# A graph network on one core: one expansion product a slot, scores ahead of the next maxima, messages at once, and a joined unpacking stage

## The chip, the cores and the metric

The kernel runs on one core of a Trainium2 chip. The number that counts is the device time of one execution in microseconds (us). Before the change the median of three runs is 8563.55 us (8562.0 to 8572.29).

## The reference, cut to what matters

Four layers run over a graph of 6250 nodes and 106250 edges, each followed by a residual and a layer norm. The change touches the first two layers.

```python
x = _layernorm(x + _L0_gnn_ref(x, ...), axis=-1)     # relation messages: sum of x[src] @ W[type] per target
x = _layernorm(x + _L1_gnn_ref(x, edge_index, ...))  # first attention
x = _layernorm(x + _L2_gnn_ref(x, edge_index, ...))  # second attention
x = _layernorm(x + _L3_gnn_ref(x, edge_index))       # routing, 6 rounds

# L1, HEADS = 4, HID = 64
h = (x @ W).reshape(n, HEADS, HID)
a_src = einsum('nhf,hf->nh', h, att_src);  a_dst = einsum('nhf,hf->nh', h, att_dst)
e = leaky_relu(a_src[src] + a_dst[dst], 0.2)
m = segment_max(e, dst, n)
ex = exp(e - m[dst])
alpha = ex / segment_sum(ex, dst, n)[dst]
agg = segment_sum(h[src] * alpha[:, :, None], dst, n)
out = relu(agg.reshape(n, HEADS * HID) + bias) @ fc_w + fc_b
```

## The kernel before, in words

Nodes lie in 49 tiles of 128. Edges are sorted on the chip into chunks of 128 slots, each chunk belonging to one target tile; there are NCH = 880 chunks, and 464 pairs of chunks (NPAIR) of which the last ones are padding that reads one same dummy row. The program is a row of phases, and between two phases stands a barrier of all engines. In each phase every engine runs its own instruction list, and semaphores order the engines.

**Start.** Tables `y_tab` are made, and GpSimd (POOL) scatters one record an edge (L296).

**Unpacking phase (L534 to L574).** SyncE (SP) loads all records into `rec` by one DMA (L546). VectorE (DVE) unpacks three columns, `dl_f` (lane of the target), `y_row` (row of `y_tab`) and `src_row`; TensorE (PE) turns `dl_f` in seven blocks, DVE copies them to `dl_t`, and SP stores that to `dl_tab`. A barrier follows.

**First pass (L694 on).** DVE clears the whole of `acc` (13000 elements a partition) and `ring`, and copies `lane` to PSUM. Only then does POOL gather rows of `y_tab`, one indirect DMA a chunk (L584), four chunks (a quad) a ring slot, four slots. PE multiplies each chunk by a one-hot matrix (`hots`, made by DVE, L652), and DVE adds the product to `acc` (L785). DVE also makes byte tables of the one-hot matrices from `dl_b`, which SP loads from `dl_tab` (L731) and stores again for the later passes.

**dense_layer (twice).** It normalizes the sums, multiplies by `fc`, adds, runs the layer norm and writes the table of the next pass. In the second call SP loads four slots of own rows (L937, 512 KB each) first, then `fc`, `h_col`, `fcb_b` and the table weights. PE waits for these weights (`s_fc`) ahead of `turn(0)`, its first transposes; `turn(g)` also waits for POOL's product of own rows `g` (`s_oh`, L1088).

**attend_running (first attention pass).** It goes over 58 places of 16 chunks (8 pairs). For each place POOL issues 16 gathers of table rows into one of three ring slots (L1356); a slot is free when the totals of the place three before have been made. The other engines work in a pipeline over two places; E is the start of the exponential of a place (ScalarE, ACT, L1557):

- maxima of place b: PE spreads the source scores of a pair (`spread`, 8 matmuls, L1626), DVE reduces them (`reduce`, L1402, 1024 elements) and takes the running maximum (`top`, L1410). Eight pairs a place. The spreads of pairs 0 to 3 need `line(b, 0)`, those of pairs 4 to 7 `line(b, 1)`, which ACT copies (L1536) from PE's `turn(b, n)` (L1612) of ACT's `pack(b, n)` (L1527).
- `shift(b)`: four DVE instructions (L1416 to L1424) make the new shift of every node, in three bf16 parts.
- `expand(b)`: PE brings target score and shift to the edges: for each of 16 chunks three accumulating matmuls of 8 columns, one a part, so 48 (L1637).
- `scores(b)`: three DVE instructions (L1455, L1458, L1461). Then ACT's two exponentials (L1557 to PSUM, L1558), then DVE's `message(b)` for one head (L1467) and ACT's `message(b, a)` for three heads (L1566, 6 instructions a pair).
- `total(b, a)`: PE sums a pair (L1654) and DVE adds it to `acc` (L1475), one place later, between the maxima of the next place.

DVE's order around a place: reduces and tops of b with adds of b-1; `shift`; the last two adds of b-1; `reduce(b+1, 0)`, `reduce(b+1, 1)` and `top(b+1, 0)`; `scores(b)`; `message(b)`; `rescale(b)` (L1443, L1446). ACT's order: exponentials of b-1; `pack(b, 1)`; `line(b, 1)`, which waits for PE's turn; the 48 message instructions of b-1; `pack(b+1, 0)`; `hot(b)`; `line(b+1, 0)`; `widen(b+1)`; `fading(b)`; exponentials of b.

## Time and profile before

| | |
|---|---|
| median of three runs | 8563.55 us |
| profiled execution, device time | 8565.55 us |
| its span in the profile | 8563.6 us |
| busy: PE, DVE, ACT, POOL | 62%, 66%, 36%, 71% of the span |
| unpacking phase and start of the first pass | 1183 to 1222 us |
| first pass | 1222 to 2353 us |
| first dense layer | 2353 to 2455 us |
| first attention pass | 2455 to 3716 us |
| second dense layer | from 3716 us |

The profile gives, for one execution, busy and idle time by engine and by group of instructions, and what released each wait. Shares over the whole span mix stages with different limits, so the stages are read one by one, in the view in order of time. Granted clock is the TensorE clock as a share of 2.4 GHz; 0.50 is the 1.2 GHz level.

### The profile page before, as it was taken

To read this page: it belongs to the slowest core of one execution; us is meant where nothing else is said; L and a number is where in the kernel's file an instruction comes from. 1 tells how busy PE (TensorE), PEld (TensorE's weight loads), DVE (VectorE), ACT (ScalarE), POOL (GpSimd) and SP (SyncE) were. 2 spreads that over 40 slices of the span, in tenths; PEclk is the share of its full clock that TensorE was granted. 3 is DMA by queue.
4 is the path that set the end of the run, shared out by engine and by line. 5 is a ranking of instruction groups with operands and counts; after the bars stand their busy time and mean duration, and the time that the engine had idled before them with its cause. 6 is when DMAs were issued, how large, how long until landed. Compare 5 with 4: busy or idle time off the path is not lost. (4 is left out here: it accounts for less than half of the span.)

```text
span 8563.6 us, 137030 instructions
## 1 busy us (share of the span) xinstructions
PE 5287.4 (62%) x37370; PEld 4671.1 (55%) x37370; DVE 5613.1 (66%) x13450; ACT 3042.1 (36%) x7001; POOL 6100.7 (71%) x5620
## 2 busy tenths in 40 slices
PE   0991014444368888763444415655579898989896
PEld 0340013333346666563333315655579898989896
DVE  9661025555578888763444455555579898989898
ACT  2000002000048888732222222222256666666564
POOL 4777767777647777727777727777768787878785
PEclk6995555555578888886666657677689999999998
DMA  1771015565645555623333324444567676767674
GB/s 43 271 308 54 2 46 130 131 145 131 118 111 139 138 136 138 123 66 79 82 79 82 79 48 130 129 129 130 123 172 221 189 222 190 222 189 222 189 222 138
DMA packets 962997, 1176.44 MB, mean 137 GB/s; under 512 B 286474, under 2 KB 845278, under 8 KB 949198
## 3 DMA queue, kind: packets, MB, share of 16 engines
q1 hardware_dynamic: 806638, 864.50, 33.2%
q0 software_dynamic: 155616, 303.19, 16.6%
q8 instruction: 326, 5.34, 0.3%
q14 instruction: 417, 3.42, 0.1%
HBM read 897.16 MB, written 269.96 MB: 136 GB/s over the span
## 5 line engine op out<-in xcount | busy, mean ns | idle before, releaser
L2572 PE MATMUL ps<-u,wide_r 128*128 x9280 | 1141.9, 277 | 128.7 <-issue 89.0
L2572 PEld LDWEIGHTS ps<-u,wide_r 128*128 128x128 f32 x9280 | 1093.6, 194 | 130.7 <-issue 130.7
L2147 POOL DMA_INDIRECT z_r<-x_tab,src_row x880 | 852.6, 969 | 417.5 <-issue 267.8
L2584 PE MATMUL ps<-msg_r,hots_r 128*128 128x128 f32 x9280 | 1135.5, 275 | 21.5 <-POOL msg_r L2405 21.5
L2405 POOL TENSOR_TENSOR msg_r<-zo_r,share_r 128x1024 f32<-128x1024 f32 x580 | 1123.1, 1936 | 11.8 <-DVE share_r L2457 9.0
L1356 POOL DMA_INDIRECT ring_e<-t_tab,src_p x928 | 878.9, 947 | 322.7 <-issue 269.7
L2584 PEld LDWEIGHTS ps<-msg_r,hots_r 128*128 128x128 f32 x9280 | 1082.6, 192 | 26.7 <-POOL msg_r L2405 25.3
L296 POOL DMA_INDIRECT rec_tab<-pay,row_i x831 | 806.3, 970 | 375.0 <-issue 274.3
L584 POOL DMA_INDIRECT ring<-y_tab,y_row x880 | 839.4, 954 | 306.0 <-issue 266.2
L2413 POOL TENSOR_TENSOR prod_r<-prod_r 128x512 f32<-128x512 f32 x580 | 735.0, 1267 | 415.9 <-DVE prod_r L2435 414.6
L1767 POOL DMA_INDIRECT ring_e<-t_tab,src_row x880 | 830.7, 944 | 271.9 <-issue 271.9
L843 PE MATMUL ps<-ring,hots 128*128 128x129 f32 x1760 | 453.2, 438 | 696.9 <-issue 548.2
L843 PEld LDWEIGHTS ps<-ring,hots 128*128 128x128 f32 x1760 | 394.1, 329 | 756.1 <-issue 649.9
L2289 PE MATMUL ps<-unit,wide_r 128*128 x1760 | 398.0, 418 | 582.9 <-ACT wide_r L2254 582.9
L2468 DVE TENSOR_TENSOR u_sum<-ps,u_sum 128x128 f32 x2320 | 670.9, 289 | 91.7 <-PE ps L2584 17.8
L2435 DVE TENSOR_TENSOR prod_r<-ps,zo_r 128x1024 f32<-128x1024 f32 x580 | 704.5, 1215 | 35.7 <-PE ps L2572 32.4
L2289 PEld LDWEIGHTS ps<-unit,wide_r 128*128 128x128 f32 x1760 | 369.5, 320 | 603.1 <-issue 603.1
L1566 ACT ACTIVATE ring_e<-ring_e 128x64 f32<-128x64 f32 x2752 | 662.2, 335 | 0.0
L2518 ACT ACTIVATE wide_r<-zo_r 128x1024 f32<-128x1024 uint8 x580 | 605.4, 1044 | 96.2 <-PE ps L2572 62.6
L1654 PE MATMUL ps<-ring_e,hots_e 128*128 128x260 f32 x1856 | 580.7, 446 | 81.1 <-ACT ring_e L1566 54.7
L1402 DVE TENSOR_REDUCE high_e<-ps 128x4 f32<-128x1024 f32 x464 | 559.6, 1216 | 69.1 <-PE ps L1626 65.4
L2535 ACT ACTIVATE hots_r<-zo_r 128x1024 f32<-128x1024 uint8 x580 | 603.3, 1040 | 0.0
(320 smaller groups left out, 9520.7 us busy)
## 6 DMA issues: line engine op xcount, KB each, us to landing
zo_r<-zo_tab SPq DMA_DIRECT2D x2320, 192.0 KB, 2.8
y_tab<-wide SPq DMA_DIRECT2D x100, 1024.0 KB, 3.9
zo_tab<-z_r SPq DMA_DIRECT2D x110, 512.0 KB
hot_bytes_e<-hb_tab SPq DMA_DIRECT2D x464, 64.0 KB
dl_b<-dl_tab SPq DMA_DIRECT2D x220, 128.0 KB, 3.8
zo_tab<-hot_bytes SPq DMA_DIRECT2D x220, 128.0 KB, 2.3
hb_tab<-hot_bytes SPq DMA_DIRECT2D x220, 128.0 KB, 2.3
hot_bytes_e<-hb_tab SPq DMA_DIRECT2D x55, 512.0 KB
```

The source lines that it names most:

```text
L296: nc.gpsimd.indirect_dma_start(out=rec_tab, out_offset=bass.IndirectOffsetOnAxis(ap=row_i[:, j:j + 1], axis=0), in_=pay[:, j, :], in_offse ...
L584: nc.gpsimd.indirect_dma_start(out=ring[:, s, c, 0:width], out_offset=None, in_=table, in_offset=bass.IndirectOffsetOnAxis(ap=rows[:, q * ...
L843: last = nc.tensor.matmul(sum_of(s, c), hots[:, s, c, :], ring[:, s, c, :], start=True, stop=True)
L1356: nc.gpsimd.indirect_dma_start(out=ring[:, b % ZR, c, :], out_offset=None, in_=t_tab, in_offset=bass.IndirectOffsetOnAxis(ap=src_p[:, b * ...
L1767: nc.gpsimd.indirect_dma_start(out=ring[:, b % ZR, c, :], out_offset=None, in_=t_tab, in_offset=bass.IndirectOffsetOnAxis(ap=src_row[:, b ...
L2147: nc.gpsimd.indirect_dma_start(out=z[:, g % ZR, c, :], out_offset=None, in_=x3_tab, in_offset=bass.IndirectOffsetOnAxis(ap=src_row[:, g * ...
L2289: last = nc.tensor.matmul(ps[:, 2 * (g % 2) + c // 4, c % 4 * D:(c % 4 + 1) * D], wide[:, g % WR, c, :], unit[:, bass.ds(tiles[at // CQ, a ...
L2405: nc.gpsimd.tensor_tensor(msg[:, g % WR].rearrange("p c (k d) -> p c k d", d=CD), z_of(g).rearrange("p c (k d) -> p c k d", d=CD), share[: ...
L2413: nc.gpsimd.tensor_tensor(prod[:, :, 0:CD // 2], prod[:, :, 0:CD // 2], prod[:, :, CD // 2:CD], ALU.add).then_inc(s_half, 1)
L2435: v.tensor_tensor(prod[:].rearrange("p (c k) d -> p c (k d)", k=CAPS), up, z_of(g), ALU.mult).then_inc(s_prod, 1)
L2572: last = nc.tensor.matmul(ps[:, 2 * (g % 2) + c // 4, c % 4 * D:(c % 4 + 1) * D], wide[:, g % WR, c, :], u[:, bass.ds(tiles[g % NO % 4 * O ...
L2584: last = nc.tensor.matmul(ps[:, 4 + g % 2, c // 2 * D:(c // 2 + 1) * D], hots[:, g % WR, c, :], msg[:, g % WR, c, :], start=c % 2 == 0, st ...
```

## The change

Four things are edited. (1) The unpacking phase is gone as a phase: its instructions move into the first pass. `rec` is loaded in two DMAs, columns 0 to 63 and the rest, and POOL's gather waits for `y_row` of the first 64 columns only (and at quad 16 for the rest) in place of the clearing. DVE clears the last column of `ring` and the first 129 columns of each `acc` tile only, behind the unpacking. (2) In the first attention pass `expand` is one matmul of 24 columns a chunk, and DVE adds the three parts in a new reduce into `sent` ahead of the scores. (3) There DVE's order becomes `scores(b)`, `reduce(b+1, 0)`, `message(b)`, `rescale(b)`, `reduce(b+1, 1)`, `top(b+1, 0)`; ACT starts the messages of b-1 right behind the exponentials, with `pack(b, 1)` ahead of pair 1 and `line(b, 1)` ahead of pair 2; PE's `turn(b, 1)` moves behind `total(b-1, 0)`. (4) In the dense layers `turn(0)` stands ahead of the wait for the first weights, and in the second call own rows 1 to 3 are loaded behind `fc`, `h_col` and `fcb_b`.

```diff
-        with Phase() as ph:
-            rec = sb("rec", [P, NCH, 4], i32, ph)
...
-                    sp.dma_start(rec[:], rec_tab[0:SLOTS, :].rearrange("(p c) w -> p c w", p=P)).then_inc(s_r, 16)
...
                 @block.sync
                 def _(sp):
+                    for n, c in enumerate((slice(0, FIRST), slice(FIRST, NCH))):
+                        sp.dma_start(rec[:, c, :], rec_tab[0:SLOTS, :].rearrange("(p c) w -> p c w", p=P)[:, c, :])\
+                          .then_inc(s_r[n], 16)
+                    sp.wait_ge(s_d, BL)
+                    for b in range(BL):
+                        rows = min(P, NCH - b * P)
+                        sp.dma_start(dl_tab[b * P:b * P + rows, :], dl_t[0:rows, b, :]).then_inc(s_o, 16)
+                    sp.wait_ge(s_o, 16 * BL)
...
                 def _(pool):
-                    pool.wait_ge(s_ini, 2)
-                    gather = gather_quads(pool, y_tab, y_row, ring, s_gath, s_sum, D)
+                    gather_rows = gather_quads(pool, y_tab, y_row, ring, s_gath, s_sum, D)
+
+                    def gather(q, s):
+                        if q % (FIRST // CQ) == 0 and q <= FIRST // CQ:
+                            pool.wait_ge(s_y, q // (FIRST // CQ) + 1)
+                        gather_rows(q, s)
...
                 def _(dve):
-                    nc.vector.memset(acc[:], 0.0).then_inc(s_ini, 1)
-                    nc.vector.memset(ring[:], 1.0).then_inc(s_ini, 1)
+                    nc.vector.memset(dl_t[:], 0.0).then_inc(s_z, 1)
+                    nc.vector.memset(ring[:, :, :, D:W], 1.0).then_inc(s_ini, 1)
                     nc.vector.tensor_copy(lane_ps, lane[:]).then_inc(s_ini, 1)
+                    for n, c in enumerate((slice(0, FIRST), slice(FIRST, NCH))):
+                        dve.wait_ge(s_r[n], 16)
+                        nc.vector.tensor_copy(y_row[:, c], rec[:, c, 0]).then_inc(s_y, 1)
+                    nc.vector.tensor_copy(dl_f[:], rec[:, :, 2]).then_inc(s_c, 1)
+                    nc.vector.tensor_copy(src_row[:], rec[:, :, 1]).then_inc(s_c, 1)
+                    nc.vector.memset(acc[:, :, 0:W], 0.0).then_inc(s_ini, 1)
...
                     if not first:
-                        for g in range(OR):
-                            own_in(g)
+                        own_in(0)
                     sp.dma_start(fc[:], fc_in.rearrange("(k d) n -> d k n", d=P)).then_inc(s_fc, 16)
...
+                        for g in range(1, OR):
+                            own_in(g)
...
+                    turn(0)
                     if first:
                         pe.wait_ge(s_wr, 1)
                     else:
                         pe.wait_ge(s_fc, 64)
-                    turn(0)
...
+                            v.tensor_reduce(sent[:].rearrange("p c w -> p (c w)"),
+                                            expanded(b).rearrange("p (c k w) -> p c w k", c=BC, k=3),
+                                            AX.X, ALU.add).then_inc(s_sent, 1)
...
-                            if b + 1 < NB:
-                                reduce(b + 1, 0)
-                                reduce(b + 1, 1)
-                                top(b + 1, 0)
...
                             if now:
                                 scores(b)
+                            if b + 1 < NB:
+                                reduce(b + 1, 0)
+                            if now:
                                 message(b)
                                 if behind:
                                     rescale(b)
+                            if b + 1 < NB:
+                                reduce(b + 1, 1)
+                                top(b + 1, 0)
...
-                            if b < NB:
-                                pack(b, 1)
-                                line(b, 1)
-                            if b >= 1:
-                                for a in range(BP):
+                            for a in range(BP):
+                                if b < NB and a == 1:
+                                    pack(b, 1)
+                                if b < NB and a == 2:
+                                    line(b, 1)
+                                if b >= 1:
                                     message(b - 1, a)
...
                             for c in range(BC):
-                                for k in range(3):
-                                    last = nc.tensor.matmul(
-                                        sent_of(b)[:, c, :], wide[:, b % WR, c, :],
-                                        sent_b[:, b % 2, bass.ds(tiles[b][c // 2], 1), k, 1:4 * HEADS:2]
-                                        .rearrange("p t w -> p (t w)"), start=k == 0, stop=k == 2)
+                                last = nc.tensor.matmul(
+                                    expanded(b)[:, c * SW:(c + 1) * SW], wide[:, b % WR, c, :],
+                                    sent_b[:, b % 2, bass.ds(tiles[b][c // 2], 1)]
+                                    .rearrange("p t k w -> p (t k w)")[:, 1:2 * SW:2], start=True, stop=True)
...
-                                    if a == 2:
+                                    if a == 3:
                                         turn(b, 1)
```

## Rows read from the trace of the kernel before

**Rows 1.** Page: busy, mean ns, idle before (part 5); KB, us to landing (6).
```profile
L584 POOL DMA_INDIRECT ring<-y_tab,y_row x880 | 839.4, 954 | 306.0 <-issue 266.2
...
zo_r<-zo_tab SPq DMA_DIRECT2D x2320, 192.0 KB, 2.8
```
**Rows 2.** In order of time, unpacking phase; start, duration (us), idle before in brackets.
```profile
1189.55 0.33 SPq L546 DMA_DIRECT2D rec<-rec_tab  x1
1196.58 0.94 DVE L558 CAST dl_f<-rec 128x880 f32<-128x880 int32 x1 [6.44 <-DMA rec<-rec_tab]
...
1205.78 1.28 SPq L731 DMA_DIRECT2D dl_b<-dl_tab  x3
1208.56 10.89 DVE L759 MEMSET acc<- 128x13000 f32 x1 [7.91 <-issue]
...
1221.88 0.97 POOL L584 DMA_INDIRECT ring<-y_tab,y_row  x1 [37.88 <-DVE ps L761]
```
**Rows 3.** The line of the gathers of the first attention pass; idle before it.
```profile
L1356 POOL DMA_INDIRECT ring_e<-t_tab,src_p x928: 940/946/1140, 2455.4 to 3639.8; - x186
...
  issue: 269.7, 885
  PE ps L1654: 36.7, 42
```
**Rows 4.** In order of time, one place of that pass.
```profile
2989.58 0.23 ACT L1557 ACTIVATE ps<-score_e 128x64 f32<-128x64 f32 x1 [2.83 <-DVE score_e L1461]
...
2990.93 11.55 ACT L1566 ACTIVATE ring_e<-ring_e 128x64 f32<-128x64 f32 x48
...
2992.51 2.10 PE L1654 MATMUL ps<-ring_e,hots_e 128*128 128x260 f32 x4 [0.93 <-ACT ring_e L1566]
...
2995.50 1.23 DVE L1402 TENSOR_REDUCE high_e<-ps 128x4 f32<-128x1024 f32 x1 [0.32 <-PE ps L1626]
...
3003.55 0.37 DVE L1416 TENSOR_TENSOR sum_n_e<-most,a_dst 128x200 f32<-128x200 f32 x1
...
3006.31 2.93 PE L1637 MATMUL ps<-sent_n_e,wide_e 128*128 x48
...
3006.82 2.34 DVE L1402 TENSOR_REDUCE high_e<-ps 128x4 f32<-128x1024 f32 x2
...
3010.04 0.23 ACT L1557 ACTIVATE ps<-score_e 128x64 f32<-128x64 f32 x1 [2.80 <-DVE score_e L1461]
```
**Rows 5.** In order of time, second attention pass: its expansion and its reduce.
```profile
3920.34 1.76 PE L1908 MATMUL ps<-exp_n_e,wide_e 128*128 x16
3922.14 0.37 DVE L1787 TENSOR_REDUCE ps<-ps 128x64 f32<-128x192 f32 x1 [2.35 <-PE ps L1908]
...
4040.97 0.93 PE L1908 MATMUL ps<-exp_n_e,wide_e 128*128 x16
```
**Rows 6.** In order of time, end of the first attention pass.
```profile
3573.16 0.94 POOL L1356 DMA_INDIRECT ring_e<-t_tab,src_p  x1 [0.85 <-PE ps L1654]
...
3656.83 1.87 PE L1626 MATMUL ps<-lines_e,pick_e 104*128 104x128 bf16 x16 [30.65 <-issue]
...
3661.61 0.23 ACT L1557 ACTIVATE ps<-score_e 128x64 f32<-128x64 f32 x1 [33.13 <-DVE score_e L1461]
...
3682.15 0.23 ACT L1557 ACTIVATE ps<-score_e 128x64 f32<-128x64 f32 x1 [2.68 <-DVE score_e L1461]
...
3702.24 0.23 ACT L1557 ACTIVATE ps<-score_e 128x64 f32<-128x64 f32 x1 [4.08 <-DVE score_e L1461]
```
**Rows 7.** Stretches: us, busy (instructions) of PE, PEld, DVE, ACT, POOL; clock, DMA share, GB/s.
```profile
3630.00:3640.00 10.00, 0.00 (x0) 0.00 (x0) 0.00 (x0) 0.00 (x0) 7.56 (x9) 0.50 1.02 97
```
**Rows 8.** In order of time, starts of the two dense layers.
```profile
2361.48 1.94 PE L1168 MATMUL ps<-ident,acc 128*128 128x128 f32 x8 [12.04 <-DVE acc L986]
3720.09 4.49 POOL L1088 TENSOR_TENSOR own_rows_d<-own_rows_d,own 128x1024 f32<-128x1024 f32 x1 [15.43 <-DMA own_rows_d<-t_tab]
3725.65 0.79 PE L1170 MATMUL ps<-ident,acc 128*128 128x128 f32 x2 [11.12 <-DMA fcb_b_d<-in_L_gnn_fc_b]
```

More of the change, by code:

```diff
@@ L705, in gnn_resnorm_kernel @@
             s_bst = [sem(f"hot_bytes_stored_0_{s}", ph) for s in range(RING)]
+            FIRST = 64
+            rec = sb("rec", [P, NCH, 4], i32, ph)
+            s_r = [sem(f"records_in_{n}", ph) for n in range(2)]
+            s_y = sem("y_rows_unpacked", ph)
+            s_c = sem("records_unpacked", ph)
+            s_z = sem("target_rows_cleared", ph)
+            s_t = sem("dl_transposed", ph)
+            s_d = sem("dl_rows_ready", ph)
+            s_o = sem("dl_rows_stored", ph)
             dl_i = sb("dl_i_0", [P, BL, P], i32, ph)
@@ L758, in _ @@
                 def _(dve):
-                    nc.vector.memset(acc[:], 0.0).then_inc(s_ini, 1)
-                    nc.vector.memset(ring[:], 1.0).then_inc(s_ini, 1)
+                    nc.vector.memset(dl_t[:], 0.0).then_inc(s_z, 1)
+                    nc.vector.memset(ring[:, :, :, D:W], 1.0).then_inc(s_ini, 1)
                     nc.vector.tensor_copy(lane_ps, lane[:]).then_inc(s_ini, 1)
+                    for n, c in enumerate((slice(0, FIRST), slice(FIRST, NCH))):
[4 more added lines that the diff above has]
+                    nc.vector.memset(acc[:, :, 0:W], 0.0).then_inc(s_ini, 1)
+                    dve.wait_ge(s_z, 1)
+                    for b in range(BL):
+                        rows = min(P, NCH - b * P)
+                        dve.wait_ge(s_t, b + 1)
+                        nc.vector.tensor_copy(dl_t[0:rows, b, :], ps[0:rows, b, 0:P]).then_inc(s_d, 1)
+                    dve.wait_ge(s_c, 2)
                     dve.wait_ge(s_ini, 3)
@@ L791, in take_bits @@
                         if q == 15:
+                            dve.wait_ge(s_d, BL)
                             nc.vector.tensor_copy(dl_i[:], dl_t[:]).then_inc(s_bit, 1)
@@ L836, in _ @@
                 def _(pe):
+                    pe.wait_ge(s_c, 1)
+                    for b in range(BL):
+                        rows = min(P, NCH - b * P)
+                        nc.tensor.transpose(ps[0:rows, b, 0:P], dl_f[:, b * P:b * P + rows], ident[:]).then_inc(s_t, 1)
+                    pe.wait_ge(s_d, BL)
                     def total(q, s):
@@ L839, in total @@
                         pe.wait_ge(s_gath[s], gathered(q, s))
+                        if q == 0:
+                            pe.wait_ge(s_ini, 3)
                         if not isinstance(q, int) or q >= 2:
@@ L1278, in attend_running @@
                 s_exp = sem(f"expanded_{name}", ph)
+                s_sent = sem(f"expanded_parts_added_{name}", ph)
                 s_sc = sem(f"scores_{name}", ph)
@@ L1304, in turned, with expanded @@
                     return ps[0:PR, 6 + b % 2, at:at + P].bitcast(bf16)
-                def sent_of(b):
-                    return ps[:, 6 + b % 2, 256:256 + BC * 2 * HEADS].rearrange("p (c w) -> p c w", w=2 * HEADS)
+                SW = 3 * 2 * HEADS
+                def expanded(b):
+                    return ps[:, 6 + b % 2, 0:BC * SW]
                 def factors(b):
@@ L1454, in scores @@
                                 dve.wait_ge(s_gath[b % ZR][n], rows_gathered(b))
-                            v.tensor_tensor(sc, sent_of(b)[:, :, 0:HEADS], ring[:, b % ZR, :, hf:W], ALU.add)\
+                            v.tensor_reduce(sent[:].rearrange("p c w -> p (c w)"),
+                                            expanded(b).rearrange("p (c k w) -> p c w k", c=BC, k=3),
+                                            AX.X, ALU.add).then_inc(s_sent, 1)
+                            dve.wait_ge(s_sent, b + 1)
+                            v.tensor_tensor(sc, sent[:, :, 0:HEADS], ring[:, b % ZR, :, hf:W], ALU.add)\
                              .then_inc(s_sc, 1)
```

39 lines of the change are left out of this document (3 added, 36 removed).

## The prediction, made before the changed kernel was run

> **What bounds the kernel now.** I read the page's groups first, to see which stages POOL's gathers pace, then the view in order of time at each place that the change touches, then the view of the gather line with what ended its waits. In the first pass 880 gathers are 839.4 us busy and 306.0 us idle, of which 266.2 is issue [rows 1]: 0.95 + 0.30 = 1.25 us a gather and next to no wait for anybody. The rest of that idle time is one wait ahead of the first gather, 37.88 us long [rows 2]. So the pass starts late, and once started it runs at POOL's own pace: only the start can be shortened.
>
> The first attention pass has 928 gathers, median 0.946 us with 0.30 us of issue, again 1.25 us, so 16 of them, a place, take 20.0 us. The exponentials of two neighbouring places stand 3010.04 - 2989.58 = 20.46 us apart [rows 4]. POOL waited 42 times for PE's totals, 36.7 us together [rows 3]: the ring was full, the compute loop is the slower one, by half a microsecond a place. POOL is the next bound right behind it. The page's shares (POOL 71%, DVE 66%) show none of this; the two periods side by side do.
>
> The end of that pass is a third case. From 3573.16 [rows 6] POOL issues the gathers of the last three places, which are padding and all read one row; that their index is the same is my reason from the code. In the stretch 3630 to 3640 no engine computes, while the DMA engines are 1.02 busy [rows 7]. PE goes on at 3656.83 [rows 6], 83.7 us after 3573.16. That stretch is paced by DMA: it shifts when its start shifts. Behind it stand three more exponentials, at 3661.61, 3682.15 and 3702.24 [rows 6], with all rows on the chip: there the compute loop alone decides.
>
> **Part 1, joined unpacking.** Before, POOL's first gather is at 1221.88 and the load of the records is issued at 1189.55; the whole takes 7.0 us to land, then come unpacking, stores, a barrier (SP goes on at 1205.78) and the clearing, until 1221.5 [rows 2]. After, the first gather needs a load of 64 columns (1 KB a partition), one copy of 64 elements and one semaphore. The small load's landing is not in the trace. Upper bound: the whole table's 7.0 us, if both pieces share the engines. Lower: 2.8 us, the median of a 192 KB load [rows 1]. I take 3.1, near the row of like size (the piece has 128 KB), and 0.2 for the copy. First gather at 1189.55 + 3.3 = 1192.9, so 29.0 us sooner; 25 with the late landing.
>
> Is it given back? Behind POOL's first 16 gathers (until 1212.9) the fifth quad waits for the first total. DVE must by then have done: second piece in at about 1197, three copies of 880 (about 0.95 each [rows 2]), the clearing, seven small copies (1.5), register loads (1.4), the one-hot quad (0.7). A memset runs longer than its row shows: idle 7.91 ahead of L759 includes about 2.8 us after SP had resumed, so 10.89 + 2.8 = 13.7 us for 13000 elements, 1.05 ns each; 50 x 129 elements take 6.8 us. That makes 1210, PE's eight matmuls 2 more: 1212.1, just under 1212.9. The byte tables wait for the stores of `dl_t` and the load of `dl_b` (about 1216), and the hot matrices of quad 2 stand behind them on DVE, about 1218, total 1220; POOL wants it at 1223. SP's loads of `dl_b` and its stores of byte tables are queued behind that same wait; nobody else waits for them. The cover is one to three microseconds deep. If it is gone, POOL loses what is lacking once, a few us, since DVE has 3.5 us of work in a quad of 5. Term: -29.0, bounds -23 and -30.
>
> **Part 2, one expansion product.** 48 matmuls take 2.93 us [rows 4], 61 ns each. Sixteen at that pace take 0.98. The second attention pass already does this with 12 columns, 16 in 1.76 or in 0.93 us [rows 5]. So 0.93 to 1.76; I take 1.0, since here two chunks share one register, as in the old form. Added is DVE's reduce of 384 to 128 elements from PSUM. 192 elements take 0.37 us [rows 5] and 1024 take 1.23 [rows 4]: 1.03 ns an element, so 0.37 + 0.20 = 0.57, with its wait 0.6. VectorE: DVE Perf Modes, Rules for kernel authors, in the Trainium skill calls the reduce on a hot path the slowest DVE operation and advises restructuring, which speaks against this edit. The slope of 1.03 ns agrees; the page's rule would reject the edit, but by these rows the reduce costs a third of what the 32 matmuls do.
>
> **Part 3, the order of a place.** Count from E = 2989.58. Before [rows 4]: first total at 2.93 (it waited for ACT's messages, which begin at 1.35), reduce of pair 3 at 5.92, shift at 13.97, expansion 16.73 to 19.66, next E at 20.46. DVE's last two reduces (2.34 us from 3006.82) end just then, so both DVE and PE held up the scores.
> After: messages begin at 0.43, pair 0 done at 2.0. DVE does reduce 0 behind the scores (until 1.2), then `message`, as long as a reduce, done at 2.4. The first total starts at 2.45, now on DVE's word. DVE goes on with rescale (0.55), reduce 1, top, reduce 2, top, add: about 6.1 for reduce 3. So the two reduces moved behind E come out of what was idle, and reduce 3 stays within 0.2 us of its old place. From there DVE goes 1.54 us a pair as before, and shift stays at 14.0. ACT's `line(b, 1)` now waits for PE's turn, queued behind the first total (about 4.5): messages 2 to 7, `hot` and `line(b+1, 0)` stand behind it, ending near 15.7 where it was 15.4. So the expansion may start 0.3 later, at 17.0, and end at 18.0; DVE is free at 17.3. Then reduce 0.6 and scores 0.8: next E at 19.4. With the expansion at 1.76 it is 20.2.
>
> So the compute loop falls from 20.46 to 19.4 (up to 20.2), under POOL's 20.0, and POOL becomes the bound. Only PE's share of the waits goes. Of the 42 waits two are at the storm of padding (7.5 and 0.7 us), and 40 contain 0.30 of issue each: 36.7 - 8.2 - 12.1 = 16.4 us. Check: 880 gathers from 2455.4 [rows 3] at 1.25 end at 3555.4, and 3573.16 is 17.8 later. For doubt about PE's clock (below) I take -15; bounds 0 and -17.8.
>
> At the end, compute-bound: 0.6 us at 3661.61, 20.54 to 19.5 for the next, and the last place, without other work behind `shift`, some 1.6: -3. A loop less far behind the gathers lets SP issue the bit loads of the next places earlier in the storm. Place 56 could start sooner, but its successor still needs the last gathers. Bounds 0 and -6, taken -1.5.
>
> **Part 4, dense layers.** In the first one PE begins at 2361.48, released by DVE's scaling of `acc` [rows 8]; the weights were there before. Nothing. In the second PE begins at 3725.65, put down to the last weights, but POOL's first product ends only at 3720.09 + 4.49 = 3724.58 [rows 8], and `turn(0)` needs it. So at most 1.1 us of the 11.12 shown; next late is POOL's chain of products. Own rows 1 to 3 are moved behind four small loads, about 2 us on SP's queue, and POOL wants the second at 3724.6: covered. Own row 0 may land sooner. -0.8, bounds +1 and -1.5.
>
> **Sum.** -29.0 - 15 - 3 - 1.5 - 0.8 = -49.3 us. The profiled execution is 8565.55 us and its sum 8516.3; the median of runs lies 2.0 lower, so 8514.
>
> **Rivals.**
> A. The loop does not get under 20.0. PE's clock: every place begins with PE at the lower level, and less expansion work plus a longer pause ahead of the next place leave it colder; the first total already takes 2.10 us [rows 4]. Against: before 3656.83 PE had been idle 30 us at granted clock 0.50, the 1.2 GHz level [rows 6 and 7], and the next place still took 3682.15 - 3661.61 = 20.54. TensorE: Matmul & The Clock Gate, Why this matters for your kernels, in the Trainium skill warns that pauses between bursts throw the clock back; the fall to 0.50 agrees, yet the 20.54 shows it costs one place only 0.1. With slow expansions or a longer wait for `line` the period is 20.0 to 20.46, part 3's gain 0 to 7: about 8525 to 8531. 20%.
> B. The storm gives more, or all bounds fall well: -30 - 17.8 - 3.5 - 6 - 1.5 = -59: 8505. 10%.
> C. The join does not bring what it says: DVE's clearing and SP's stores now stand behind running gathers, POOL stalls in the first quads for some 10 us, and part 3 is as forecast: 8525. 6%.
> D. Slower. Two more pairs of each place at the lower clock. A cold pair costs PE 2.10 for the total and 1.87 / 2 = 0.94 for the spread [rows 4 and 6], 3.0 against DVE's 1.54: +1.5 us. From 19.7 one cold pair gives 21.2, or +0.74 x 57 = +42, which cancels the other gains; two give +3.0, 22.7, so 57 x 2.24 = +128, less 33: 8658. It decides from one more cold pair on. Little speaks for it. 3%.
>
> **Chances.** Forecast 61%, A 20%, B 10%, C 6%, D 3%. The range must reach A and C; 8500 to 8532 holds the forecast, its bounds, most of A, B and C. A measurement of this kernel can tell about 0.2%, 17 us, from no change. Faster by more: forecast, B, C and nearly all of A, 94%; within: 3%; slower: 3%.
>
> **What would show it.** First gather some 29 us sooner after the load of the records, and no PE wait in the first quads. In the attention pass no wait of POOL for PE's totals up to the padding, exponentials 19.98 us apart, a DVE reduce near 0.57, 16 expansions near 1.0. Exponentials 19.4 apart behind the storm. PE in the second dense layer released by POOL. The prediction is wrong if the period stays above 20.2, if the early quads stall POOL, or if the storm takes another time than 84 us.

## The result, and the profile after

The changed kernel takes 8514.31 us (median of four runs, 8512.61 to 8515.75) against 8567.15 us before; the ratio is 0.9940, with a 95% interval of 0.9928 to 0.9952. Forecast were 8514 us and "faster by over 0.2%", and both hold. (One of the eight executions of kernel e2 below took 10478 us at a granted clock of 0.72, where the others had 0.75 to 0.76; its ratio leaves that one out, and its cause is not known.) The profiled span fell from 8563.6 to 8510.8 us, by 52.8. This budget is made from the starts of single instructions in the two traces, and it adds up. The first dense layer is counted from the first load of its weights. The 881st gather is the first of the 48 that are padding:

| stretch | before | after | difference |
|---|---|---|---|
| start to the load of the records (unchanged code) | 1189.6 | 1187.2 | -2.4 |
| load of the records to first gather | 32.3 | 2.5 | -29.8 |
| first gather to the first dense layer | 1134.0 | 1137.1 | +3.1 |
| first dense layer | 99.5 | 99.8 | +0.3 |
| attention pass, first to 881st gather | 1117.7 | 1105.4 | -12.3 |
| 881st gather to first load of own rows | 143.1 | 134.1 | -9.0 |
| second dense layer, to the next pass's first gather | 131.4 | 129.3 | -2.1 |
| the rest (unchanged code) | 4716.0 | 4715.4 | -0.6 |

**The start**, kernel after, view in order of time (start, duration in us, engine, line; idle before in brackets), to be held against [rows 2]:

```profile
1187.18 0.80 SPq L695 DMA_DIRECT2D rec<-rec_tab  x2
1189.21 0.22 DVE L743 COPY y_row<-rec 128x64 int32<-128x64 int32 x1 [1.21 <-DMA rec<-rec_tab]
1189.70 0.97 POOL L541 DMA_INDIRECT ring<-y_tab,y_row  x1 [8.06 <-DVE y_row L743]
...
1198.38 5.43 DVE L746 MEMSET acc<- 128x6450 f32 x1 [1.29 <-PE ps L833]
...
1208.32 1.60 DVE L776 TENSOR_TENSOR acc<-ps,acc 128x129 f32 x4 [1.72 <-PE ps L844]
...
1213.09 0.48 DVE L763 TENSOR_SCALAR hot_bytes<-dl_b,part 128x512 uint8<-128x512 bf16 x1 [3.17 <-DMA dl_b<-dl_tab]
```

The small load lands 2.0 us after its issue, POOL starts 0.5 us later, and DVE clears and unpacks while the gathers run. DVE already adds the first products at 1208.3, when POOL has issued 15 of the 16 gathers that it may issue without them.

**The gathers of the attention pass**, kernel after, the view of their line (duration min/median/max in ns, first and last start; then POOL's idle time before them in us and how often), for [rows 3]:

```profile
L1362 POOL DMA_INDIRECT ring_e<-t_tab,src_p x928: 942/947/1199, 2426.6 to 3591.1; - x186
...
  issue: 280.7, 921
...
  PE ps L1666: 1.8, 6
...
  ACT slot_parts_e L1539: 143.5, 61
```

POOL's 42 waits for PE's totals, 36.7 us [rows 3], are 6 with 1.8 us, each no longer than an issue (0.30). The last row is the other side: ACT now waits 143.5 us in 61 waits for gathered rows, where it waited 24.1 us in 5 before. Compute has become the one that waits.

**One place**, kernel after, in order of time, for [rows 4]:

```profile
2944.96 0.73 PE L1649 MATMUL ps<-sent_n_e,wide_e 128*128 x16
2945.73 0.56 DVE L1461 TENSOR_REDUCE sent_e<-ps 128x128 f32<-128x384 f32 x1 [0.17 <-PE ps L1649]
2947.11 0.23 ACT L1569 ACTIVATE ps<-score_e 128x64 f32<-128x64 f32 x1 [1.21 <-DVE score_e L1471]
2949.43 2.07 PE L1666 MATMUL ps<-ring_e,hots_e 128*128 128x260 f32 x4
```

The expansion takes 0.73 us where it took 2.93 (medians over the pass 0.66 and 2.91), the reduce 0.56. From place 3 to place 53 the exponentials stand 20.12 us apart on average (20.48 before), single ones 18.9 to 23.3.

**The end of the pass**, kernel after, in order of time, for [rows 6]; and two stretches (us, busy and instructions of PE, PEld, DVE, ACT, POOL; granted clock, DMA share, GB/s), for [rows 7]:

```profile
3554.83 0.23 ACT L1569 ACTIVATE ps<-score_e 128x64 f32<-128x64 f32 x1 [1.87 <-DVE score_e L1471]
3614.09 0.23 ACT L1569 ACTIVATE ps<-score_e 128x64 f32<-128x64 f32 x1 [32.32 <-DVE score_e L1471]
3633.05 0.23 ACT L1569 ACTIVATE ps<-score_e 128x64 f32<-128x64 f32 x1 [1.08 <-DVE score_e L1471]
3651.33 0.23 ACT L1569 ACTIVATE ps<-score_e 128x64 f32<-128x64 f32 x1 [2.47 <-DVE score_e L1471]
```

```profile
3531.00:3591.00 60.00, 32.69 (x200) 24.39 (x200) 33.03 (x68) 33.22 (x113) 45.45 (x48) 0.67 0.96 94
3591.00:3611.00 20.00, 0.60 (x7) 0.63 (x8) 0.00 (x0) 0.00 (x0) 0.94 (x1) 0.50 1.00 86
```

The storm of padding is still there: 59 us between two exponentials, with DMA at 0.96 to 1.00 of its time for 90 GB/s. Behind it stand the loop's own periods, 18.96 and 18.28 us (the last place has no successor's maxima to work on). By the first of them compute could run a place a full microsecond faster than POOL lets it; that is an estimate from one place.

### The profile page after: what moved, and what is told of

Read it like the earlier page. It is cut to its first block and busy times, and to the rows that moved or that the text cites. A ratio compares the mean times of both kernels' runs of the same rounds, so it can differ in the third digit from the quotient of the medians.

```text
span 8510.8 us, 132427 instructions
## 1 busy us (share of the span) xinstructions
PE 5215.0 (61%) x35514; PEld 4581.5 (54%) x35514; DVE 5632.1 (66%) x13509; ACT 3045.4 (36%) x7001; POOL 6107.9 (72%) x5620
## 5 line engine op out<-in xcount | busy, mean ns | idle before, releaser
L2447 DVE TENSOR_TENSOR prod_r<-ps,zo_r 128x1024 f32<-128x1024 f32 x580 | 704.4, 1214 | 35.6 <-PE ps L2584 32.3
L1666 PE MATMUL ps<-ring_e,hots_e 128*128 128x260 f32 x1856 | 615.0, 466 | 43.1 <-ACT ring_e L1578 22.1
```

The lines of the kernel that those rows point to most:

```text
L2447: v.tensor_tensor(prod[:].rearrange("p (c k) d -> p c (k d)", k=CAPS), up, z_of(g), ALU.mult).then_inc(s_prod, 1)
```

## The experiments

Two theories were to be told apart. Mine: part 1 takes the 30 us that stood ahead of the gathers, parts 2 and 3 together bring the compute loop under POOL's pace, and neither does it alone. Against it: the expansion or the order alone carries the gain, or PE's clock decides (rival A and D). A second question came from the profile after: what the storm is.

All twelve experiments, with the ratio to the kernel before on the same chip. They ran on three chips, so compare ratios rather than medians. "Period" is the mean distance of the exponentials from place 3 to place 53, "pass" goes from the first gather of the attention pass to the first load of own rows, "tail" from its last gather to that load.

| kernel | median us | ratio (95% interval) | period | pass | tail |
|---|---|---|---|---|---|
| before | 8563 to 8568 | 1 | 20.48 | 1260.8 | 76.4 |
| after | 8514.31 | 0.9940 (0.9928 to 0.9952) | 20.12 | 1239.5 | 75.0 |
| e1 part 1 alone | 8536.92 | 0.9961 (0.9947 to 0.9974) | 20.48 | 1259.1 | 73.1 |
| e2 parts 2 and 3 | 8547.94 | 0.9974 (0.9963 to 0.9985) | 20.12 | 1237.5 | 73.2 |
| e3 part 4 alone | 8562.44, one run | | 20.48 | 1247.8 | 55.8 |
| e4 part 2 alone | 8629.71 | 1.0065 (1.0051 to 1.0079) | 21.62 | 1321.4 | 83.4 |
| e5 part 3 alone | 8570.61 | 1.0002 (0.9993 to 1.0011) | 20.70 | 1257.8 | 63.5 |
| e6 e4, expansions three times | 8622.13 | 1.0067 (1.0054 to 1.0081) | 21.63 | 1308.9 | 64.8 |
| e10 e4, filled pause | 8601.90 | 1.0047 (1.0033 to 1.0060) | 21.36 | 1305.3 | 76.3 |
| e7 after, expansions twice | 8509.85 | 0.9939 (0.9925 to 0.9952) | 20.08 | 1238.6 | 76.1 |
| e11 after, scores behind the maxima | 8525.82 | 0.9958 (0.9945 to 0.9972) | 20.49 | 1247.0 | 61.8 |
| e12 after, messages later | 8529.05 | 0.9960 (0.9947 to 0.9974) | 20.07 | 1244.1 | 78.4 |
| e8 after, blank sources spread | 8444.09 | 0.9862 (0.9847 to 0.9877) | 20.12 | 1200.1 | 34.1 |
| e9 e8, and blank `y_tab` rows | 8429.89 | 0.9844 (0.9830 to 0.9857) | 20.11 | 1196.8 | 31.9 |

The last column is a warning. From the last gather on it is 55.8 us in one kernel and 76.4 in another whose code up to there is the same (e3 and before). Part of that is only where the last gather falls: counted from the 881st gather it is 129.3 and 143.1 us, so 14 us apart. Behind the pass, from the first gather of the second attention pass to the end, unchanged code takes 4714.0 to 4723.8 us (all kernels but e8 and e9). The runs of the kernel before itself lie between 8551.58 and 8577.84 us. So I read effects in the attention pass from the period first and from the medians second. There is one trace a kernel; how far the tail moves between executions of one kernel is not shown.

### Part 1 alone (e1)

The edit is the diff's first part, without the others.

> The kernel before with part 1 alone (the record unpacking joined to the first message pass). Theory (the 30 us of unpacking stood ahead of an unbroken row of gathers, and what the unpacking still issues on the vector engine hides behind them): first gather about 30 us sooner, the 816 gathers of the pass at their old pace of 1.25 us a gather with no wait of the pool engine near the moved steps, attention pass untouched at 20.46 us a place; 8535 to 8540 us. Rival C (the hot quads are late once the row-copies stand ahead of them): about 10 us come back as waits of POOL between gathers 8 and 60, 8545 to 8550. Rival of the measured span (the profiled after began its gathers slower by 3 us): 8538.

Measured: 8536.92 us, ratio 0.9961. From the load of the records to the first gather 2.6 us, from there to the last gather of the pass 1106.1 us (before 1106.6), to the dense layer 1134.2 (1134.0). (The pass has 880 gathers, not the 816 of my expectation.) Nothing is given back; rival C falls, and the 3.1 us that the kernel after loses in this stretch do not come with part 1.

### Parts 2 and 3 together (e2)

> The kernel before with parts 2 and 3 (one expansion product and a reduction in place of three products; new order on DVE, ACT and PE), unpacking and dense layers as before. Theory (POOL's 16 gathers of 1.25 us, 20.0 to 20.1 us a place, are the bound once the compute loop is under it): period 20.1 us, the pass ends 18 to 22 us sooner, 8545 to 8549 us. Rival (the gain of the pass came from gathers that start at another time against the unpacking, not from the loop): under 5 us, 8562 or more.

Measured: 8547.94 us, ratio 0.9974, period 20.12. The same view of the gather line, kernel e2:

```profile
L1360 POOL DMA_INDIRECT ring_e<-t_tab,src_p x928: 942/946/1187, 2453.3 to 3617.6; - x186
...
  PE ps L1664: 4.9, 16
```

From first to last gather 1164.3 us, in the kernel after 1164.5, before 1184.4. The two ratios, 0.9961 and 0.9974, multiply to 0.9935, against 0.9940 for all together: within the intervals, the parts add up.

### The expansion alone (e4): the change that would have failed

```diff
-                                for k in range(3):
-                                    last = nc.tensor.matmul(
-                                        sent_of(b)[:, c, :], wide[:, b % WR, c, :],
...
+                                last = nc.tensor.matmul(
+                                    expanded(b)[:, c * SW:(c + 1) * SW], wide[:, b % WR, c, :],
...
+                            v.tensor_reduce(sent[:].rearrange("p c w -> p (c w)"),
```

> The kernel before with part 2 alone: one expansion product and a DVE reduction in place of three products, in the old order. Theory (in the old order DVE comes to the scores after its reductions of the next place's maxima, and not after PE; the shorter expansion ends behind their cover and the added reduction of 0.57 us is all on the chain): period 20.9 to 21.1 us, 8590 to 8605 us, slower than the kernel before by 25 to 40. Rival (PE's expansion is what the scores wait for; 48 matmuls take 1.2 us more than 16 and a reduction): period 19.3 to 20.1, 8545 to 8550.

Measured: 8629.71 us, slower than before by 0.65%, and beyond what I expected: a period of 21.62 us, in a pattern over three places of 22.3, 21.5 and 21.0. Kernel e4 in order of time, PE, with one row of DVE:

```profile
3015.28 0.74 PE L1644 MATMUL ps<-sent_n_e,wide_e 128*128 x16
3018.12 0.55 DVE L1459 TENSOR_REDUCE sent_e<-ps 128x128 f32<-128x384 f32 x1
...
3020.17 0.41 PE L1620 MATMUL ps<-ident_b,slot_parts_e 128*48 128x128 bf16 x2 [4.15 <-ACT slot_parts_e L1535]
...
3022.47 2.10 PE L1661 MATMUL ps<-ring_e,hots_e 128*128 128x260 f32 x4 [0.93 <-ACT ring_e L1574]
...
3025.22 1.44 PE L1661 MATMUL ps<-ring_e,hots_e 128*128 128x260 f32 x4
...
3043.46 2.10 PE L1661 MATMUL ps<-ring_e,hots_e 128*128 128x260 f32 x4 [0.93 <-ACT ring_e L1574]
...
3046.21 2.05 PE L1661 MATMUL ps<-ring_e,hots_e 128*128 128x260 f32 x4
...
3048.90 1.55 PE L1661 MATMUL ps<-ring_e,hots_e 128*128 128x260 f32 x4
```

Two things are to be seen. The expansion is done at 3016.0, but DVE reaches the reduce only at 3018.12, behind its two reductions of the next maxima: PE's gain buys nothing, and the reduce comes on top. And PE now stands idle for 4.15 us ahead of the turn. Kernel before, the same wait:

```profile
3010.67 0.41 PE L1612 MATMUL ps<-ident_b,slot_parts_e 128*48 128x128 bf16 x2 [1.44 <-ACT slot_parts_e L1527]
```

Behind the pause up to three totals of a place take 2.10, 2.05 and 1.55 us, where the later ones take 1.10. The place that starts at 3019.54, with 2.10 and 1.44, lasts 20.99 us; that is before's 20.46 [rows 4], whose first two totals take 2.10 and 1.46, plus 0.53 for the reduce. The next place, whose slow totals hold 1.06 us more, lasts 22.3, which is 1.3 more. So of the 1.14 us that e4 loses a place, some 0.5 are the reduce and 0.6 the slow totals; this is an estimate from these two places and the average. The slow totals lie where the clock is low. The same kernel, stretches of these two places:

```profile
3020.00:3025.90 5.90, 4.80 (x24) 3.68 (x25) 3.58 (x7) 5.40 (x23) 4.68 (x5) 0.50 0.47 118
3026.00:3039.00 13.00, 10.00 (x93) 7.81 (x92) 12.00 (x25) 10.69 (x32) 9.06 (x10) 1.00 0.47 123
3040.00:3049.80 9.80, 7.71 (x36) 6.00 (x37) 6.18 (x12) 8.77 (x38) 7.30 (x8) 0.50 0.50 131
```

The granted clock is 0.50 for some 6 us of the place of 20.99 us and for some 10 us of the one of 22.3. This is the mechanism of rival D, at nearly its price (1.5 us a slow pair), in a kernel where it decides.

### Is it the pause? (e6, e10)

Both start from e4 and give PE more work that changes no result: every expansion three times, or 60 small products that nobody reads behind the expansions.

```diff
-                            for c in range(BC):
+                            for c in [*range(BC)] * 3:                # e6
...
+                            for _ in range(60):                       # e10
+                                nc.tensor.matmul(ps[:, 6 + (b + 1) % 2, 448:512], ident_b[:], ident_b[:, 0:64],
+                                                 start=True, stop=True)
```

> The kernel of e4_expand (part 2 alone, old order) with every expansion product issued three times, so 32 more matmuls a place with the same result. In e4_expand PE stands idle 4.2 us between the 16 expansions and the next turn, and 2 to 3 of the next pairs' totals take 1.4 to 2.1 us instead of 1.1; in the kernel before, with 48 expansions, it stands 1.4 us and 1.5 totals are slow. Theory (what made part 2 alone cost 61 us is 0.57 us of reduction a place plus PE thrown back to 1.2 GHz by the longer pause): the added work shortens the pause to about 2.6 us, the first totals are faster again, period 20.9 to 21.1 us instead of 21.6, 8595 to 8605 us: faster by about 30 than the same kernel without the added work. Rival (the pause does not matter and the added matmuls are cost or neutral): 8629 us or more.

> The kernel of e4_expand (part 2 alone, old order) with 60 matmuls of 64 columns that nobody reads, issued right after the expansions of a place, in the pause in which PE there stands idle for 4.2 us; e6_warm had shortened that pause to 3.5 us only, since its 48 products take 1.45 us, and had changed nothing in the pattern of 22.4, 21.5 and 21.0 us a place. Theory (61 us of part 2 alone are 0.57 us of reduction a place, 32 us, and 0.6 us a place of totals at the lower clock after the pause, 34 us): with the pause filled every place takes 20.9 to 21.1 us or less, 8585 to 8600 us. Rival (the clock has nothing to do with it, and the pattern over three places has another cause, such as the ring of three): the pattern stays, 8620 to 8630.

Measured for e6: 8622.13 us, period 21.63, no change. Its 48 products take 1.45 us and not 2.9, so the pause is still 3.3 to 3.5 us and not 2.6. The forecast failed; the test was too weak to decide, and taken alone it speaks for the rival. For e10: 8601.90 us, period 21.36, pass 1305.3 against 1321.4 us. Kernel e10 in order of time, PE:

```profile
2924.59 1.91 PE L1650 MATMUL ps<-ident_b 128*128 128x64 bf16 x60
2928.94 0.29 PE L1620 MATMUL ps<-ident_b,slot_parts_e 128*48 128x128 bf16 x2 [2.44 <-ACT slot_parts_e L1535]
2929.16 0.62 PE L1634 MATMUL ps<-lines_e,pick_e 104*128 104x128 bf16 x8
2931.13 2.10 PE L1664 MATMUL ps<-ring_e,hots_e 128*128 128x260 f32 x4 [1.35 <-ACT ring_e L1574]
```

and the stretch 2600 to 3500 us, first of e4, then of e10:

```profile
2600.00:3500.00 900.00, 646.28 (x4822) 500.27 (x4821) 722.03 (x1501) 691.27 (x2363) 636.37 (x670) 0.79 0.50 130
```

```profile
2600.00:3500.00 900.00, 705.23 (x7400) 563.80 (x7399) 727.43 (x1521) 701.18 (x2397) 639.82 (x677) 0.88 0.50 131
```

With 60 useless matmuls a place the granted clock rises from 0.79 to 0.88 of 2.4 GHz, the first spread behind the pause falls from 1.03 to 0.62 us, and the period by 0.27 us: 57 x 0.27 = 15. (The pass gets 16 us shorter, but 7 of these lie in its tail, and the intervals of the two ratios overlap; the period is the surer figure.) Work that can only delay PE made the loop faster while the clock rose: that shows that the clock costs time here and that PE's idle time has a part in it. TensorE: Matmul & The Clock Gate, Why this matters for your kernels, in the Trainium skill says that idle gaps between bursts take the clock back to the lower level; the rise to 0.88 agrees. Yet less than half of the 0.6 us came back: the forecast of 20.9 to 21.1 us in every place failed, as did the rival's unchanged pattern. The first total still takes 2.10 us, and places of 22.3 remain. In the rows above PE waits 2.44 us, works 0.8, waits 1.35, and the total behind that runs at 0.50. What decides how long the clock then stays low stays open, and so what the rest of e4's slow totals would need.

### The order alone (e5)

```diff
-                                reduce(b + 1, 0)
-                                reduce(b + 1, 1)
-                                top(b + 1, 0)
...
                                 scores(b)
+                            if b + 1 < NB:
+                                reduce(b + 1, 0)
```

> The kernel before with part 3 alone: scores ahead of the next maxima, messages at once, the second turn one step later, with the old 48 expansion matmuls. Theory (the two parts need each other: with the scores moved ahead, DVE stands waiting for the 48 matmuls): period 20.3 to 20.6 us, 8562 to 8570 us, within 5 us of the kernel before. Rival (the order alone carries the gain, since the maxima's 1.5 to 2 us leave the chain whatever the expansion takes): period 20.1, bound by POOL, 8545 to 8550 us.

Measured: 8570.61 us, ratio 1.0002 (0.9993 to 1.0011), period 20.70, a tenth above my upper end. Kernel e5, DVE, in order of time:

```profile
3014.70 0.23 DVE L1455 TENSOR_TENSOR score_e<-ps,ring_e 128x64 f32<-128x64 f32 x1 [2.89 <-PE ps L1640]
```

DVE stands 2.89 us waiting for the 48 matmuls, the time in which it used to do the two reductions. Part 2 without part 3 is slower, part 3 without part 2 changes nothing, both together gain 0.26%, 22 us. They are one change.

### How deep is POOL's cover? (e7, e11, e12)

Three kernels from the kernel after: the expansions issued twice (`[*range(BC), *range(BC)]`, same result); the scores behind both maxima again; the messages later and the turn earlier again.

> The kernel after with every expansion product issued twice: 16 more matmuls a place, about 0.7 us, on the compute loop's chain (the scores wait for the last of them). Theory (the pass is bound by POOL's 16 gathers of 1.256 us, 20.1 a place, and the compute loop has about 1 us of slack under it): period 20.1 to 20.2, 8513 to 8520 us. Rival (the loop is still bound by its own chain, whose mean is the 20.12 us seen): period 20.8, 57 x 0.7 = 40 us more, 8554.

> The kernel after with one piece of part 3 undone: DVE again takes both next maxima ahead of the scores; the messages at once and the later turn stay. Theory (the scores' place on DVE carries part 3): period 20.4 to 21.0, compute-bound again, 8530 to 8565 us. Rival (POOL's 20.1 would hide this too): 20.1, 8514.

> The kernel after with the other piece of part 3 undone: ACT again packs and copies the second half ahead of the messages, and PE turns it one step sooner; the scores stay ahead of the maxima. The first message starts about 0.9 us later after the exponential, the loop's own period is 19.0 plus 0.5 to 0.9. Theory: still under POOL's 20.1, so no change, 8512 to 8520 us, and only the last two places without gathers take 19.5 to 19.9 instead of 19.0. Rival (the loop's mean is what sets the period): 20.6 to 21.0, 8540 to 8560.

e7: 8509.85 us, period 20.08, with the expansions doubled. The doubling was weaker than planned: the median expansion takes 1.06 us against 0.66, so 0.4 us more and not 0.7. Kernel e7, one of them in order of time, then its gather line:

```profile
2960.36 1.03 PE L1649 MATMUL ps<-sent_n_e,wide_e 128*128 x32
2961.43 0.56 DVE L1461 TENSOR_REDUCE sent_e<-ps 128x128 f32<-128x384 f32 x1 [0.47 <-PE ps L1649]
```

```profile
  PE ps L1666: 7.3, 24
...
  ACT slot_parts_e L1539: 124.6, 61
```

The scores do wait for the added products, and the period does not move; ACT's wait for rows shrinks from 143.5 to 124.6 us instead. POOL is the bound, with at least these 0.4 us to spare. e11: period 20.49, POOL waits again; the same view of the gather line, kernel e11:

```profile
L1362 POOL DMA_INDIRECT ring_e<-t_tab,src_p x928: 940/946/1103, 2427.4 to 3612.7; - x186
...
  PE ps L1664: 36.6, 39
```

These are before's waits [rows 3] to a tenth. So without the new place of the scores the loop does not get under POOL. It was also a surprise the other way: e11's pass is e4's with the messages at once and the later turn, and has 20.49 where e4 has 21.62. These two do take the loss of part 2 away; POOL's bound hides what more they do.

One caution goes with e11. Its period is before's almost to the hundredth, as e1's and e3's are, and the clock records of these four traces are alike too: between 2600 and 3500 us each has 44 stretches of 6.8 us at granted clock 0.50 and 44 of 13.7 us at 1.00 in turn, and one of each makes 20.5 us, a place. The kernels at 20.1 us show no such regular change. Whether the loop carries the clock along or is held by it, no run tells. So 20.49 less 20.12 is not the price of the scores' place; that place is needed, and its size stays open.

e12 has a period of 20.07 as expected, and the last two places take 18.69 and 19.06, where I had said 19.5 to 19.9. Its median is 8529.05, above my 8520, for no reason that I find in the pass: of the 11.8 us between its profiled span and that of the kernel after, 5.9 lie behind the first gather of the second attention pass, 2.3 ahead of the first gather of all, 3.4 in the tail. By the medians alone e11 (0.9958) and e12 (0.9960) can't be told apart; the two differ in the period, and e11's tail of 61.8 us hides that.

### Part 4 alone (e3)

> The kernel before with part 4 alone (order of loads and the first turn in the dense layers). Theory: nothing in the first dense layer; in the second the first matmul is released by POOL's product and no longer by the weights, and the stretch from the first load of own rows to the first table product is 0 to 1.5 us shorter; the time stays within the noise, 8560 to 8570 us.

Kernel e3 in order of time, to be held against [rows 8]:

```profile
3713.86 0.77 PE L1171 MATMUL ps<-ident,acc 128*128 128x128 f32 x2 [10.20 <-POOL own_rows_d L1089]
...
3744.07 1.90 POOL L1089 TENSOR_TENSOR own_rows_d<-own_rows_d,own 128x1024 f32<-128x1024 f32 x1 [3.55 <-DMA own_rows_d<-t_tab]
```

PE starts 8.5 us after the first load of own rows (before 9.4), released by POOL, as forecast. From that load to the first table product it is 94.9 us, as before: later POOL waits 3.5 us for each load of own rows, which fits loads that set the pace. The 2.1 us that the kernel after gains in the stretch are not part 4's: e6, without part 4, has 93.3 us to the table product as the kernel after has, and e12, with it, 94.9.

### What the storm is (e8, e9)

Blank records all name node `NT * P`. In e8 partition p names `NT * P + p`, a row of the same dummy tile; in e9 the `y_tab` column names row `p * R` too. No real edge is touched.

```diff
-                    v.memset(pay[:, 0:NCH // 2, 1:2], NT * P).then_inc(s_blank_made, 1)
+                    link(v.tensor_scalar(far[:], part[:, 0:1], float(NT * P), None, ALU.add))
+                    v.tensor_scalar(pay[:, 0:NCH // 2, 1:2], pay[:, 0:NCH // 2, 1:2], far[:, 0:1], None, ALU.add)\
+                     .then_inc(s_blank_made, 1)
...
-                                out=src_f[:], in0=src_p[:].rearrange("p (a c) -> p a c", c=2), scalar=float(-NT * P),
-                                in1=pair_ok[:], op0=ALU.add, op1=ALU.mult).then_inc(s_own, 1)
+                                out=src_f[:], in0=src_p[:].rearrange("p (a c) -> p a c", c=2), scalar=far[:, 0:1],
+                                in1=pair_ok[:], op0=ALU.subtract, op1=ALU.mult).then_inc(s_own, 1)
```

> The kernel after, where the blank records name 128 different dummy source rows (one per partition) instead of one and the same, in all passes that gather source rows: first and second attention pass and routing. The values computed for real edges are the same. Theory (the last gathers of each pass, all padding, read one row 128 times, and that is why the DMA engines run at share 1.0 at 40 to 60 GB/s and the last rows land 20 us late): the attention pass ends about 18 us sooner, the second attention pass and the routing gather about 12 each, 8465 to 8480 us, and the DMA share in the last 50 us of the attention pass is 0.5 to 0.6 as in its middle. Rival (the share of 1.0 has another cause, such as the gathers of three free ring slots going out together): no change, 8514.

> As e8_spread_src, and the blank records also name 128 different rows of the table of the first message pass. Theory: the first pass too, whose last 35 us run at DMA share 1.0, ends about 15 us sooner than in e8_spread_src, 8450 to 8465 us. Rival (the first pass is paced by the stores of the hot matrices at its end and not by the gathers' reads): as e8_spread_src.

e8 takes 8444.09 us and e9 8429.89, ratio 0.9844 (0.9830 to 0.9857): faster than before by 134 us, and by 84 than the changed kernel (82 by the ratios). Both lie under the range that I expected, by 21 and 20 us: the direction was right and the size was not. Kernel e8, the two stretches that are shown of the kernel after above:

```profile
3531.00:3591.00 60.00, 47.62 (x348) 35.62 (x348) 51.78 (x109) 49.99 (x171) 44.04 (x47) 0.81 0.44 121
3591.00:3611.00 20.00, 13.69 (x87) 10.42 (x88) 15.75 (x34) 15.46 (x59) 1.93 (x1) 0.76 0.00 1
```

The same number of gathers with the same bytes; DMA falls from 0.96 to 0.44 of its time and moves more. (My expectation spoke of 40 to 60 GB/s in the storm; it is 86 to 94.) Reading one row from all 128 partitions is the storm, and nothing else was changed. In the kernel after, the last 48 gathers are issued from 3532 on and DMA is busy all the time until 3611, some 1.65 us each, against POOL's 1.26. The tail is 34.1 us for 75.0. I had forecast 18 us here, by the wait for the last rows alone, and it is 39 (pass 1239.5 to 1200.1): the places behind the rows had been held up as well, and in e8 they run beside the gathers. The other two passes gain 11.6 and 13.0 us (forecast 12 each), the first pass 16.4 in e9 (forecast 15). Its last stretch, kernel after and then e9:

```profile
2255.00:2300.00 45.00, 14.25 (x56) 12.53 (x56) 19.16 (x47) 0.00 (x0) 34.16 (x36) 0.50 0.84 87
```

```profile
2255.00:2300.00 45.00, 18.73 (x73) 16.36 (x74) 24.27 (x62) 0.00 (x0) 32.80 (x35) 0.50 0.54 128
```

## Why the prediction was right, point by point

- **Part 1, -29.0.** Measured -29.8, and alone (e1) 29.7. The landing of the small load was bounded between 2.8 and 7.0 us; it took 2.0, below both. The clearing was priced at 6.8 us from a memset of 13000 elements and idle time ahead of it. Its row shows 5.43 us, but 1.29 us of idle time stand ahead of it too, and in the code no wait stands between it and the copy before: together 6.72 us, 1.04 ns an element, so the price was right. DVE adds the first total 21.1 us after the load's issue, where the sum had it ready after 22.6, and POOL's 17th gather comes at 1210.7: a cover of 2.4 us where I had 0.8.
- **Part 2.** Expansion 1.0 forecast, 0.73 measured in the place shown, under the lower bound of 0.93; reduce 0.57 forecast, 0.56 measured. The premise that the reduce pays for itself because it costs a third of what the 32 matmuls do is not what decides: in the old order the same exchange lost 0.65% (e4), since PE's saving lay beside DVE's work and the reduce did not. VectorE: DVE Perf Modes, Rules for kernel authors, in the Trainium skill calls the reduce the slowest operation of DVE and advises restructuring where it is on a hot path. Followed here, that advice would have been right in the old order and wrong in the new one.
- **Part 3, the period.** The loop was worked out at 19.4 (up to 20.2); its own period behind the storm is 18.96 and 18.28, and 18.9 at its fastest. In that place of 18.96 the expansion starts 16.9 us after the exponential (forecast 17.0) and takes 0.61, and 1.4 us later the next exponential starts, as forecast: only the expansion was shorter. POOL became the bound, as said. What was off is the pace of the gathers: I took 1.25 us, and the 880 took 1.256 each (1105.4 / 880), which eats 5.4 of the 17.8 us and leaves -12.3. The -15 had been set for another doubt, PE's clock.
- **End of the pass, -4.5.** Measured -9.0. Here the prediction was wrong in what it took as fixed: it shifted the storm as a block of 84 us, and named another length as a sign of being wrong. That sign came: from the 881st gather (3532.02) to PE's going on (3610.40) it is 78.4 us where it was 83.7. What is left, -3.7, is near the -3 of the compute-bound places (20.54 to 18.96 and 20.09 to 18.28 us). The storm is no block: from the 881st gather to the third exponential from the end it takes 88.5 us before, 85.2 in e1 and 73.8 in e3, with the same code in the pass, so neither the forecast nor the measurement of this term means much.
- **Part 4, -0.8.** Nothing at the end of the stretch. PE's start did move by 0.9 us (e3); the forecast asked what is late next and answered with POOL's products, but looked at the first one only and not at the loads that all later ones wait for.
- **Sum.** -49.3 against -52.8. Behind the difference of -3.5 stand larger ones that partly cancel: -2.4 and -0.6 in unchanged code, -0.8 in part 1, +3.1 in gathers that e1 does not have, +2.7 in part 3, -4.5 at the end of the pass, -1.3 in the second dense layer. That 8514 was hit to the microsecond is luck.
- **Rivals.** A did not happen: period 20.12. C did not: no stall. B, at 8505, lay as far from the result as the scatter of this kernel reaches. D was given 3% as "little speaks for it". In the changed kernel that holds for the time, but not because the totals stayed fast: they take 466 ns a matmul where they took 446. With the old order the same expansion does lose time (e4). The 20.54 us after a cold start, which was my evidence against it, showed one place behind one long pause and said nothing of a pause in every place.

## What to carry to other kernels

When several engines stand side by side at the end of a step, shortening one buys nothing and may cost: take the order and the size together, and ask of the engine made faster how long it will then stand and what clock it comes back with. Find the bound behind the present one before counting a gain (here POOL's 20.1 under the loop's 20.48; what the loop could do below that, 0.4 us at least by e7, is unused). And look at padding as real work: let blank entries of a gather name different rows. Here that was worth some 80 us, more than the whole change.

## What the runs showed of the hardware that was not expected

- An indirect gather in which all 128 partitions read the same row keeps the DMA engines at 0.96 to 1.00 busy for 86 to 94 GB/s, some 1.65 us a gather (estimate above); over 128 different rows of equal size the share is 0.44 at 121 GB/s. Why is not known.
- A load of 64 columns of the records (1 KB a partition, 128 KB) landed in 2.0 us, less than the 2.8 us median of 192 KB loads [rows 1].
- Sixteen independent products of 24 columns took 0.73 us and 48 of them 1.45 (e6), while the 48 accumulating ones of 8 columns had taken 2.93 [rows 4]. What makes the difference no run separates.
- A memset's row can be shorter than the time it keeps DVE: 6450 elements show 5.43 us behind 1.29 us of idle time with nothing to wait for; 2064 elements in the kernel before show 1.78 behind 0.38. With the idle time both come to 1.04 to 1.05 ns an element.
- Matmuls that nobody reads made a loop faster: 60 a place took 0.27 us off a period of 21.62 (e10).
